# Graph layers and attention on one core: edge attributes moved in between the counting, table and adjacency matmuls, softmax a block further ahead, layer matmuls with the operands exchanged

## The reference

```python
cur = acc = x
for _ in range(3):
    cur = segment_sum(edge_weight[:, None] * cur[dst], src, n)
    acc = acc + cur
x = layernorm(x + acc)
h = x @ W_node.T;  e = edge_attr_64 @ W_edge.T          # 4 heads of 32
att = leaky_relu(a_src*h[src] + a_tgt*h[dst] + a_edge*e)   # sum over the head's 32, slope 0.2
w = softmax of att over each target's edges (absent edges count as 0)
x = layernorm(x + segment_sum(w * h[src], dst, n))
```

## Time and profile before

| | us |
|---|---|
| median of 3 runs | 1869.33 (1863.49 to 1871.24) |
| profiled execution | 1875.85 |
| its span | 1874.1 |
| granted TensorE clock, mean | 0.847 |
| busy: PE, PEld, DVE, ACT, POOL | 1410.6, 1099.2, 1008.1, 611.2, 103.5 |

### The profile page before, as it was taken

How to read it: one execution, slowest core, us unless ns; L and a number is a source line. 1 busy time by engine, 2 the same in 40 slices (tenths; PEclk the granted TensorE clock), 3 DMA queues, 4 the chain that set the end, 5 groups by cost and what they waited for, 6 DMA issues and landing times.

```text
span 1874.1 us, 63741 instructions
## 1 busy us (share of the span) xinstructions
PE 1410.6 (75%) x28181; PEld 1099.2 (59%) x28182; DVE 1008.1 (54%) x1574; ACT 611.2 (33%) x1526; POOL 103.5 (6%) x123
## 2 busy tenths in 40 slices
PE   3399999755544799999999488865777777777774
PEld 2399999644443344444444388864555665656663
DVE  8812222498886000200200589977777777777784
ACT  0022222344443000000000400006676676666674
POOL 0051200000000000000000000010000000000000
PEclk9999655677777899999999789997888888888887
DMA  6032422177777986486585065530000000000001
GB/s 194 1 114 98 148 93 93 32 175 173 173 173 177 355 304 239 175 307 219 186 307 208 22 225 205 202 108 19 15 15 15 15 15 15 15 15 15 15 3 36
DMA packets 129741, 230.11 MB, mean 123 GB/s; under 512 B 22984, under 2 KB 109543, under 8 KB 121222
## 3 DMA queue, kind: packets, MB, share of 16 engines
q1 hardware_dynamic: 116614, 215.11, 35.2%
q0 software_dynamic: 4000, 8.20, 1.6%
q10 hardware_dynamic: 8928, 3.72, 0.8%
HBM read 179.08 MB, written 47.91 MB: 121 GB/s over the span
## 4 chain that ended last, share of the span: by engine, by line
PE 51%; DVE 14%; SPq 12%; issue 7%; ACT 7%; DVEq 7%; DMA 1%; ACTq 0%; POOL 0%; POOLq 0%
PE bank L614 22%; SPq L284 11%; PE bank L725 8%; PE bank L532 8%; PE bank L711 5%; PE bank L523 5%; ACT pt L914 4%; DVE z_sb L1309 4%; DVE oh_lo L1009 3%; DVE qhw L1363 3%; DVEq L1362 2%; DVE osT L1296 2%; DVEq L1298 2%; ACT wt L904 1%; DVEq L1321 1%
## 5 line engine op out<-in xcount | busy, mean ns | idle before, releaser
L614 PE MATMUL bank<-ablk,cur 128*128 128x512 f32 (+1 forms) x1050 | 405.8, 550 | 23.9 <-DMA ablk<-adj 21.9
L914 ACT COPY pt<-bank 128x400 f32<-128x400 f32 x800 | 329.5, 525 | 144.2 <-PE bank L711 144.1
L711 PE MATMUL bank<-qhw,qh_s 64*128 64x104 f16 x6400 | 230.2, 226 | 162.0 <-ACT pt L914 88.7
L614 PEld LDWEIGHTS bank<-ablk,cur 128*128 128x128 f32 x1050 | 189.2, 191 | 240.7 <-issue 238.2
L711 PEld LDWEIGHTS bank<-qhw,qh_s 64*128 64x128 f16 x6400 | 180.5, 105 | 212.1 <-ACT pt L914 134.4
L1139 DVE COPY curT<-bank 128x512 f32<-128x512 f32 (+1 forms) x21 | 13.0, 633 | 416.8 <-PE bank L614 416.7
L593 PE MATMUL bank<-oh_s,ohw 64*26 64x128 bf16 x9600 | 126.5, 280 | 115.8 <-ACT at L831 95.7
L1363 DVE TENSOR_TENSOR qhw<-qhb,wt 128x3328 f16<-128x3328 f16 x100 | 189.3, 1893 | 7.8 <-issue 0.4
L593 PEld LDWEIGHTS bank<-oh_s,ohw 64*26 64x26 bf16 x9600 | 113.5, 110 | 129.3 <-issue 126.0
L725 PE MATMUL bank<-pt,hx 128*32 128x128 f32 x5000 | 181.5, 308 | 0.8 <-ACT pt L914 0.8
L532 PEld LDWEIGHTS bank<-wedge,eaT 128*128 128x128 f32 (+1 forms) x832 | 177.5, 314 | 1.4
(11 more groups left out here) (164 smaller groups left out, 1243.9 us busy)
## 6 DMA issues: line engine op xcount, KB each, us to landing
ablk<-adj SPq DMA_DIRECT2D x65, 1600.0 KB, 7.7
adj<-at SPq DMA_DIRECT2D x200, 208.0 KB
srow<-row_d SPq DMA_DIRECT2D x26, 992.0 KB, 4.9
ea<-in_edge_attr SPq DMA_DIRECT2D x25, 992.0 KB, 6.8
brow<-row_d SPq DMA_DIRECT2D x26, 248.0 KB, 5.5
ee_d<-eet ACTq DMA_DIRECT2D x13, 124.0 KB, 2.6
z_d<-z_sb ACTq DMA_DIRECT2D x26, 62.0 KB, 3.1
out<-cur SPq DMA_DIRECT2D x2, 768.0 KB
```

The lines of the kernel that those rows point to most:

```text
L614: m = pe.matmul(bank[g][:, 0:w], cur[:, b, :], ablk[:, u, g * BANK:g * BANK + w], start=(n == 0 and u == 0), stop=(n == NR - 1 and u == RI ...
L711: m = pe.matmul(bank[(g % 2) * 2 + hf][:, v * (H * B1):(v + 1) * (H * B1)], qh_s[r, q % 2, t, :], qhw[r, q % 2, t, k * H:(k + 1) * H, :].r ...
L914: m = act.copy(pt[:, par, :, :, d0:d0 + 4], bank[(g % 2) * 2 + hf][:, 0:4 * H * B1] .rearrange("p (v h b) -> p h b v", v=4, h=H)[:, :, 0:N ...
```

## The change

- `ea`, `eaT` and `eet` get memory of their own beside the one-hots of the counting and the adjacency; `eaT` has three buffers. `xs` goes; x is loaded into `acc`.
- The edge attributes are cut into steps: `edge_turn` (four transposes of step n), `edge_sum` (the matmuls of step n-1). Of the 104 steps 16 lie between the chunks of the counting, 24 ahead of and between the tables, and 64 in the adjacency loop: 8 with each three blocks, behind the bursts named in PLACES. The loop's body is six blocks on all engines that take part. SP issues a group's load behind every third block's stores.
- A layer's matmul has a 128x128 block of the adjacency stationary and the features moving, 625 a layer. Nothing has to be turned back. Banks are zeroed by seven matmuls a layer, since four blocks share one. The features of the layers alternate between `cur` and `curT`. A layer starts with its first row when six or seven of the seven copies are done.
- In attention `scores` and `exps` are made two blocks ahead, at the end of a step, and the weights are turned behind the second quarter.

```diff
-ER = 4
+ER = 3
+EARLY, INA, HISTN = 5, 8, 16
+PLACES = (0, 1, 3, 4, 6, 7, 9, 10)
...
+        def stack(l):
+            return cur if l % 2 == 0 else curT[:, :].rearrange("p (b n) -> p b n", b=NB)
...
+            def edge_turn(g, half, par, ci, last=False):
+                if ci == 0:
+                    pe.wait_ge(s[f"ea{par}"], half * 32 + (48 if last else 32))
+                need = g * NC + freed(ci)
+                if not isinstance(need, int) or need > 0:
+                    pe.wait_ge(s["eaT_sb"], need)
+                for n, (k, u, w) in enumerate(CHUNKS[ci]):
+                    m = pe.transpose(bank[EB[ci % ER]][0:w * DE, n * P:(n + 1) * P],
+                                     ea[:, par, k, u:u + w, :].rearrange("p u d -> p (u d)"), ident[:, :])
+                m.then_inc(s["eaT_ps"], 1)
+
+            def edge_sum(g, ci):
+                if ci == 0 and not (isinstance(g, int) and g == 0):
+                    pe.wait_ge(s["ee_sb"], g)
+                pe.wait_ge(s["eaT_sb"], g * NC + (ci + 1))
...
+                m.then_inc(s["eaT_used"], 1)
...
                 m.then_inc(s["hist_used"], 1)
+                if c == 1:
+                    pe.wait_ge(s["wt_sb"], 1)
+                if c % 3 and c < NH - 1:
+                    edge_steps(n, n + 1)
+                    n += 1
...
+            def fast_tables():
+                left = EARLY * NC - HISTN
+                first_steps = left - 4 * (NJB - 1)
+                n = HISTN + first_steps
+                edge_steps(HISTN, n)
+                for i in range(NJB):
+                    tables(i)
+                    if i < NJB - 1:
+                        edge_steps(n, n + 4)
+                        n += 4
...
-                with pe.Fori(0, NB) as j:
-                    half_block(j, 0)
-                    half_block(j, 1)
+                def three_rows(j, g, half, par, last=False):
+                    for k in range(12):
+                        rows(j + k // 4, k % 4 // 2, k % 2)
+                        if k in PLACES:
+                            edge_step(g, half, par, PLACES.index(k), last)
+
+                with pe.Fori(0, INA // 2 - 1) as i:
+                    three_rows(i * 6, i * 2 + EARLY, i + EARLY // 2, 1)
+                    three_rows(i * 6 + 3, i * 2 + (EARLY + 1), i + (EARLY + 1) // 2, 0)
...
                             for g, bs in enumerate(groups):
-                                m = pe.matmul(bank[g][:, 0:w], cur[:, b, :], ablk[:, u, g * BANK:g * BANK + w],
-                                              start=(n == 0 and u == 0), stop=(n == NR - 1 and u == RING - 1))
+                                if n == 0 and u == 0:
+                                    pe.matmul(bank[g][:, 0:len(bs) * P], identb[:, :], zerob[:, 0:len(bs) * P], start=True, stop=False)
+                                for k, b in enumerate(bs):
+                                    m = pe.matmul(bank[g][:, k * P:(k + 1) * P], ablk[:, u, b * P:(b + 1) * P],
+                                                  source[:, j, :], start=False, stop=(n == NR - 1 and u == RING - 1 and k == len(bs) - 1))
...
-                    for g, bs in enumerate(groups):
-                        pe.wait_ge(s["lay_sb"], l * len(groups) + (g + 1))
-                        for k, b in enumerate(bs):
-                            m = pe.transpose(bank[g][:, k * P:(k + 1) * P], curT[:, b * P:(b + 1) * P], ident[:, :])
-                        m.then_inc(s["lay_T"], 1)
...
             def step(j, par, head=False, end=False):
                 for q in range(NQ):
-                    if q == NQ - 1 and not end:
+                    quarter(j, q)
+                    if q == 1 and not end:
                         turn_weights(j + 1)
-                    quarter(j, q)
...
+                def three_rows_out(j, jhalf, jpar, g, half, par):
+                    for k in range(12):
+                        m = k // 4
+                        rows_out(j + m, jhalf + (jpar + m) // 2, (jpar + m) % 2, k % 4)
+                        if k in PLACES:
+                            edge_out(g, PLACES.index(k))
+                            if k == PLACES[0]:
+                                group_out(g - 1, half if par else half - 1, 1 - par)
...
-            def step(j, par, head=False, end=False):
+            def step(j, par, head=False, ahead=2):
                 quarter_out(j, 0, par)
-                if not end:
-                    exps(j + 1)
                 quarter_out(j, 1, par)
+                if ahead > 0:
+                    weights(j + 1, 1 - par)
                 quarter_out(j, 2, par)
-                if not end:
-                    weights(j + 1, 1 - par)
                 if not head:
                     feature_out(j - 1, 1 - par)
                 quarter_out(j, 3, par)
+                if ahead > 1:
+                    exps(j + 2)
...
                 quarter(j, 0, par)
-                if not end:
-                    scores(j + 1, 1 - par, n)
+                if ahead > 0:
+                    split_weights(j + 1)
                 quarter(j, 1, par)
-                quarter(j, 2, par)
                 if not head:
                     finish(j - 2, par)
-                if not end:
-                    split_weights(j + 1)
+                quarter(j, 2, par)
                 quarter(j, 3, par)
+                if ahead > 1:
+                    scores(j + 2, par, n)
```

More of the change, by code:

```diff
@@ L309, in any_layers @@
             def any_layers():
+                for g in range(4, NG):
+                    attr_when_free(g)
                 sp.wait_ge(s["g_init"], 5)
@@ L500, in _, with edge_step, edge_steps @@
                       start=True, stop=True).then_inc(s["wt_ps"], 1)
+            def edge_turn(g, half, par, ci, last=False):
[12 more added lines that the diff above has]
+                pe.wait_ge(s["eaT_sb"], g * NC + (ci + 1))
+                for n, (k, u, w) in enumerate(CHUNKS[ci]):
+                    m = pe.matmul(bank[7][:, (k * SH + u) * H:(k * SH + u + w) * H],
+                                  eaT[0:w * DE, ci % ER, n * P:(n + 1) * P], wedge[0:w * DE, 0:w * H],
+                                  start=True, stop=True)
+                m.then_inc(s["eaT_used"], 1)
+            def edge_step(g, half, par, ci, last=False):
+                edge_turn(g, half, par, ci, last)
+                if ci:
+                    edge_sum(g, ci - 1)
+                elif not (isinstance(g, int) and g == 0):
+                    edge_sum(g - 1, NC - 1)
+            def edge_steps(n0, n1):
+                for n in range(n0, n1):
+                    g, ci = divmod(n, NC)
+                    edge_step(g, g // 2, g % 2, ci, g == NG - 1)
+            n = 0
             for c in range(NH):
@@ L802, in _, with edge_out @@
-            for g in range(NG):
-                group(g)
-            act.wait_ge(s["ee_out0"], 16 * (NG - NG // 2))
-            act.wait_ge(s["ee_out1"], 16 * (NG // 2))
-            act.nop().then_inc(s["edge_done"], 1)
+            def edge_out(g, ci):
+                act.wait_ge(s["eaT_ps"], g * NC + (ci + 1))
+                need = g * NC + freed(ci)
+                if not isinstance(need, int) or need > 0:
+                    act.wait_ge(s["eaT_used"], need)
+                units = CHUNKS[ci]
+                full = sum(w == 2 for _, _, w in units) * P
+                m = act.copy(eaT[:, ci % ER, 0:full], bank[EB[ci % ER]][:, 0:full])
+                if full < len(units) * P:
+                    m = act.copy(eaT[0:DE, ci % ER, full:full + P], bank[EB[ci % ER]][0:DE, full:full + P])
+                m.then_inc(s["eaT_sb"], 1)
@@ L808, in fast_layers, with edge_outs @@
+            def edge_outs(n0, n1):
+                for n in range(n0, n1):
+                    g, ci = divmod(n, NC)
+                    edge_out(g, ci)
+                    if ci == 0 and g:
+                        group_out(g - 1, (g - 1) // 2, (g - 1) % 2)
+            edge_outs(0, HISTN)
             def fast_layers():
+                edge_outs(HISTN, EARLY * NC)
                 for f in range(2):
@@ L831, in block_out @@
                         act.copy(at2[:, par, n0:n0 + BANK], bank[q % AB][:, :]).then_inc(s["at_sb"], 1)
[L832 to L845 removed]
+                    if k == 3:
+                        act.drain()
+                        act.sem_inc(s["at_full"], 1)
@@ L942, in fast_attention @@
                     step(i * 2 + 2, 0)
-                step(NB - 2, 1)
-                step(NB - 1, 0, end=True)
+                step(NB - 2, 1, ahead=1)
+                step(NB - 1, 0, ahead=0)
                 feature_out(NB - 1, 0)
```

301 lines of the change are left out of this document (151 added, 150 removed).

## The result

| | before | changed |
|---|---|---|
| median of 4 runs, us | 1866.41 (1857.93 to 1871.24) | 1800.5 (1798.81 to 1807.02) |
| ratio | | 0.9652 (95% interval 0.9621 to 0.9683) |
| span of the profiled execution, us | 1874.1 | 1800.2 |
| granted clock, mean | 0.847 | 0.847 |

The account below looks back on a forecast made before the run. Stages bound in turn: counting by VectorE, edge attributes and layers by TensorE, adjacency by stores, attention by engine turns. From 1875.85 us, -101 + 3 - 22 = -120 gave 1756, or 1750 on the median's scale; range 1675 to 1815.

Parts of the forecast that it names:

- Counting: Counting stage: 16 edge steps fit in, chunks still every 2.83 us; 2 us charged at the start (0 to 8).
- Tables: Ahead of the adjacency: 24 remaining edge steps and the tables' turns put the first adjacency matmul at 174 us.
- The adjacency loop: Adjacency stage with 64 edge steps: 40 us for three blocks, bounds 31 and 50; gain 101 us with earlier stages.
- TensorE's sum of 39.8: Adjacency loop, three blocks at the slow clock: bursts 16.4 us, eight edge steps 20.2, tile changes 3.2.
- the 3.2 for the 16 changes: Adjacency loop, three blocks: 16 changes between small tiles and full array at up to 0.2 us each.
- the stores no bound: Adjacency loop: stores with the attributes on the same queue need 36 us for three blocks, below the 40 taken.
- rival 2: Adjacency loop: code loading bounds it, 44 to 50 us for three blocks, 1806 us in all; chance 0.14.
- 10.2 pieces of 4.24 us: Adjacency loop: three blocks' 2,550 instructions as pieces of code, 43 us if each were waited for.
- Layers: Three layers with the adjacency stationary: 1250 instructions a layer at 0.109 us; +3 us in sum (-5 to +12).
- The boundary: Between layers: 3.7 us of copies and transposes become one copy of 0.7; -6 us for two.
- Rival 3: Layers: loads not hidden, 0.21 us an instruction, 788 against 409 us, 2129 us in all; chance 0.04.
- Attention: Attention: cast wait of 3.3 us goes, 1.8 and 0.6 charged back; 0.9 a block, gain 22 us (0 to 60).

Follow-up runs that it names:

- the six-block loop: The kernel before with TensorE's adjacency loop written out six blocks a turn, no edge steps among them; 1971.8 us against 1873.3.
- The order alone: The kernel before with only attention's part changed: scores and exponentials two blocks ahead, weights turned behind the second quarter; 1848.3 us, ratio 0.9864.
- theory C: Claim that where piece boundaries fall in attention's code costs time; kernel before with 84 or 168 more real TensorE instructions ahead of attention: ratio 0.9922 both.

## Why the prediction was right and wrong

The measured 1800.5 us lie in the range of 1675 to 1815, 50 us above the forecast of 1750. The loop lost 60 us against its forecast, the layers 9, and the other rows brought back 22, of which attention gave 16. Some 11 of these 16 had no term in the sum, so a part of the nearness is luck.

**Counting: right.** `oh_lo` still starts every 2.83 us (23.23, 26.07 in the chain), so 16 steps went in for nothing. **Tables: right.** The first adjacency matmul stood at 172.1 us, 174 forecast.

**The adjacency loop: the step that failed.** It was 40 us for three blocks where 46.5 came, 52 of the 60 us by which the stage was off; the 25th block with what ends it took 14.5 us instead of 7. Its terms were right one by one. TensorE's sum of 39.8 is 36.5 of work: bursts and steps as priced, and of the 3.2 for the 16 changes nearly nothing came. The slow clock was right (0.56), the stores no bound, as forecast. What failed is the sentence that the limits "share nothing that adds them up", with its companion that code loading "runs beside TensorE's work" and must show only between two bursts. I had put the steps' slack against the bursts' need as means over three blocks. But three blocks have four pairs of bursts in a row. Each pair wants 384 instructions in 3 us, some 1.5 pieces, which take 6 to 7 us to come at the 4.0 to 4.5 us between pieces (4.04 in the six-block loop, which was always short of code; 4.5 here, which is also the loop's time over its 86 pieces and so no measure of supply alone). How far ahead code is read no run shows; it was less than a pair. The experiment with a step behind every burst supports this: without pairs the terms come near the time (31.7 of 34.6 us for two blocks with eight steps). So rival 2 held in its mechanism and its size (44 to 50 us, 1806 against 1800.5 measured), at a chance of 0.14 that was too low. The rows for it stood there: 10.2 pieces of 4.24 us, or 43 us, was already above the 40 I took. The largest of several limits is a lower bound, and the sum should have had something on top.

The rule that a change of tile mode drains TensorE (the Trainium skill, "TensorEngine Tiling (Array Packing)", Key Properties) costs nothing one could build on here: under 0.1 us for the two changes around a step (3.96 against 3.90), and fewer changes made it worse.

**Layers: mechanism right, size at the edge.** 12 us slower, 3 forecast, -5 to +12 the bounds. About 5 us of it come back right behind, where nothing has to be turned back: from the last layer matmul to the first of the norm it is 13.3 us instead of 18.2. With them the layers cost 7 us. The chain shows a long stretch:

```profile
588.86 134.07 PE bank L679 x1200
```

That is 0.1117 us an instruction. I had taken 0.109 from 25 transposes; over 3750 instructions the 0.0027 are 10 us. The boundary is as forecast (0.8 and 0.1 us instead of 3.7 and 3.8). The row of the kernel before was the nearer one: 350 instructions in 134.60 us over 160,000 columns (25 rows of 3,200, each in two instructions) are 0.1077 us for 128, so a load for every 128 columns costs about 0.004 us an instruction. Rival 3 fell: loads of 128 columns over all rows stay hidden, at 0.112 and not 0.21 us, against the Trainium skill's statement, in its part on packing small matmuls, that a load overlaps only in other row groups ("TensorE: Matmul & The Clock Gate", What overlaps and what doesn't).

**Attention: the order right, the rest not foreseen.** The order alone gave 25 us, 22 forecast. Its terms stand too: the wait on the cast is gone from the list, and putting the exponentials back (with the split and the scores) won 1.3 us a block (21.53 to 20.24), where 1.8 had been charged for them. Behind the layers the changed kernel gains 43.5 us. Beside the order's 25 some 5 lie ahead of attention, 2 behind it, and 11 in attention itself (529.2 us against 539.9 with the order alone). The prediction said nothing of these 11. They go with a missing pause: "issue" is 31.9 us in 10 waits in the changed kernel, 42.0 in 20 in the kernel before and with the order alone. That the code's new place took the pause away is likely after the experiments on theory C, not shown. Without the 11 us the kernel would have come out near 1811.

**Of what would show it**: the waits on "issue" and the instruction packets throughout the loop were listed, and were what the trace had most of; it was only their price that was missing.

## What to carry to other kernels

Before writing out a loop body, count its instructions: here some 1,560 of TensorE stayed loaded, 1,900 (attention) and 4,600 didn't, and writing out the adjacency loop alone cost nearly 100 us. If the body must be long, lay slow work behind every fast burst rather than behind two of three, so that code comes in nearer to the pace at which it is used; that won 15 and 8 us of 385 here. And where limits with near values share one engine's time in turns, add something to the largest, for a queue that serves the mean does not serve the burst.

## What the runs showed of the hardware

- TensorE's code came in pieces of 16 KB (some 250 instructions by the earlier trace rows), 4.04 us apart as mean in the six-block loop and 4.5 in the changed kernel's, with the DMA engines busy for 0.57 of the time in both. Bursts on small tiles, 96 matmuls in 1.41 us from one start to the next, use one in some 1.8 us.
- 84 useless instructions ahead of a loop made the kernel 0.8% faster (ratio 0.9922, 0.9895 to 0.995). In its odd blocks a pause of 1 us went, and with it a stretch of product at the low clock level (72 matmuls in 4.07 against 2.17 us); the even blocks got as much slower, so the way by which it became faster is open.
- f32 loads of 128x128 with 128 columns moving: 0.1117 us for each instruction over 1200 in a row at 2.4 GHz, against 0.1077 for 128 of up to 512 columns behind one load; the load is hidden but for some 0.004 us.
- In the changed loop, edge steps (full tiles, f32) and bursts in turns, TensorE was busy for 301 of 390 us, and the granted clock was 0.56 as mean, so mostly 1.2 GHz. In the six-block loop without any edge step, with its pauses for code, it was 0.51, and in the kernel before 0.73.
